# A GRU scan on one core: the candidate's second products with both state halves at once, the low half of r times h ahead of the update gate's additions, and the conditions' products one pair later

## What is computed

```python
xz, xr, xh = x @ W_z, x @ W_r, x @ W            # for all steps
vz, vr, vh = cond @ C_z + b_z, cond @ C_r + b_r, cond @ C + b   # once
def step(h, xs):
    z = sigmoid(xz_t + h @ U_z + vz)
    r = sigmoid(xr_t + h @ U_r + vr)
    hh = tanh(xh_t + (r * h) @ U + vh)
    return (1 - z) * h + z * hh
```

## Time and profile before

| | before |
|---|---|
| median of 3 runs | 1507.63 us |
| the profiled execution | 1507.41 us, span 1505.6 us |
| PE busy | 1499.5 us, 22917 matmuls |
| PEld busy | 1173.5 us, 98 ns for one fp16 load |
| DVE busy | 1259.6 us |
| ACT busy | 1173.0 us |
| POOL busy | 315.4 us |
| granted TensorE clock | full speed (2.4 GHz) in every slice |

### The profile page before, as it was taken

The page is one execution under the profiler, slowest core; times in us unless marked ns, Lnnn a source line. Parts: engine busy times, 40 slices in busy tenths (PEclk is TensorE's granted clock), DMA queues, the critical chain, the costliest instruction groups (busy, mean ns, idle before and its releaser), DMA issues.

```text
span 1505.6 us, 54107 instructions
## 1 busy us (share of the span) xinstructions
PE 1499.5 (100%) x22917; PEld 1173.5 (78%) x22917; DVE 1259.6 (84%) x2548; ACT 1173.0 (78%) x2726; POOL 315.4 (21%) x332
## 2 busy tenths in 40 slices
PE   9999999999999999999999999999999999999998
PEld 7874444444444467779999999999999999999998
DVE  7999999999999887777877787778887887776677
ACT  7989999999999835767777777777777777867444
POOL 1100112111110014322222222222222222222222
PEclk9999999999999999999999999999999999999999
DMA  5156465565638979533333333333333333320000
GB/s 199 40 157 194 90 192 140 133 160 142 182 87 133 143 113 102 72 53 23 49 20 48 48 21 48 42 27 47 21 47 48 20 49 20 49 41 3 32 32 31
DMA packets 545106, 116.61 MB, mean 77 GB/s; under 512 B 520160, under 2 KB 527200, under 8 KB 536160
## 3 DMA queue, kind: packets, MB, share of 16 engines
q1 hardware_dynamic: 537424, 82.14, 31.4%
q0 software_dynamic: 7008, 30.41, 11.0%
q10 hardware_dynamic: 432, 0.59, 0.1%
HBM read 66.47 MB, written 33.55 MB: 66 GB/s over the span
## 4 chain that ended last, share of the span: by engine, by line
PE 99%; DVE 0%; issue 0%; ACT 0%; DVEq 0%
PE ps L1553 33%; PE ps L1618 22%; PE ps L1655 20%; PE ps L1667 15%; PE ps L1639 6%; PE ps L1571 2%; PE ps L1510 0%; PE ps L1520 0%; PE ps L1584 0%; DVE ST L1382 0%; DVE AR L1349 0%; ACT ST L943 0%; DVE RL L1439 0%; DVE HL L981 0%; DVE HL L1486 0%
## 5 line engine op out<-in xcount | busy, mean ns | idle before, releaser
L1553 PE MATMUL ps<-XH,WH 128*128 128x512 f16 x1872 | 404.7, 379 | 0.0
L1553 PEld LDWEIGHTS ps<-XH,WH 128*128 128x128 f16 x1872 | 182.9, 98 | 220.2 <-issue 0.3
L1655 PE MATMUL ps<-HL,U 128*128 128x64 f16 x6112 | 219.8, 193 | 0.6 <-ACT ps L775 0.6
L1779 POOL TENSOR_TENSOR ST<-ST 128x256 f32<-128x256 f32 x126 | 114.5, 908 | 491.1 <-ACT ST L935 491.1
L1667 PE MATMUL ps<-HL,U 128*128 128x64 f16 x4064 | 213.9, 206 | 0.0
L1655 PEld LDWEIGHTS ps<-HL,U 128*128 128x128 f16 x6112 | 203.6, 98 | 7.1 <-ACT ps L775 0.7
L1667 PEld LDWEIGHTS ps<-HL,U 128*128 128x128 f16 x4064 | 183.1, 98 | 0.1
L1655 PEld LDWEIGHTS ps<-RL,U 128*128 128x128 f16 x4064 | 135.1, 98 | 6.1 <-issue 0.8
L1655 PE MATMUL ps<-RL,U 128*128 128x64 f16 x4064 | 139.2, 193 | 0.0
L903 ACT ACTIVATE ST<-ps,dn 128x128 f32<-128x128 f32 x252 | 78.1, 360 | 70.4 <-PE ps L1667 70.4
L950 ACT ACTIVATE HL<-ST 128x128 f16<-128x128 f32 x208 | 53.3, 302 | 80.4 <-DVE ST L1478 80.4
(11 more groups left out here) (215 smaller groups left out, 3116.4 us busy)
## 6 DMA issues: line engine op xcount, KB each, us to landing
x_scratch<-AR SPq DMA_DIRECT2D x16, 1024.0 KB, 5.3
AR<-in_x POOLq DMA_DIRECT2D x15, 1024.0 KB, 8.1
AR<-HB POOLq DMA_DIRECT2D x11, 1024.0 KB, 7.0
raw<-x_scratch SPq DMA_DIRECT2D x88, 128.0 KB, 4.4
out_y<-raw SPq DMA_DIRECT2D x11, 1024.0 KB, 4.1
raw<-in_x SPq DMA_DIRECT2D x10, 1024.0 KB, 7.4
ST<-in_x SPq DMA_DIRECT2D x5, 1024.0 KB, 7.2
out_y<-AR SPq DMA_DIRECT2D x4, 1024.0 KB, 4.2
```

The costliest lines, as they stand in the source:

```text
L1553: op = pe.matmul(ps[b][:, :], v[:, g, wp, k, e * P:(e + 1) * P], y[:, xp, k, :], start=n == 0, stop=n == 11)
L1655: pe.matmul(ps[b][:, col:col + B], U[:, g, half, k, e * P:(e + 1) * P], S[:, k, 0], start=opens, stop=False, skip_group_check=True)
L1779: pool.tensor_tensor(zc, zc, Hst[(t + 1) % 2], ALU.mult).then_inc(s_zch, 1)
```

## The change

Three edits.

1. In steps 16 to 119 C takes the joint form too (`summed_pair`): 16 matmuls of 64 columns with the low weights, then 16 of 128 columns with the high weights and both halves of `RL`. The two parts of a sum lie side by side in PSUM. `put_x` writes half the projection into both parts (512 elements of a partition, not 256). DVE adds the parts (`add_pair`, a `tensor_reduce` with two elements in each sum, one for each bank) into SBUF, and ACT takes tanh from there with the same scale. `add_pair` stands in DVE's list behind the side work of the middle of the step.
2. In steps 8 to 111 DVE makes the low half of r*h ahead of the two additions of Z.
3. `C_PAIR` is {14, 18, 22}: the conditions' products stand one pair later.

```diff
-        C_PAIR = {13: 1, 17: 2, 21: 0}
+        C_PAIR = {14: 1, 18: 2, 22: 0}
...
-            return g == 0 and not held(t, g)
+            return g == 0 and not held(t, g) or summed_pair(t, g)
...
+        def summed_pair(t, g):
+
+            return g in SUMMED and SUMMED_FROM <= t < HELD_TO
...
+                if summed_pair(t, g):
+                    both = PS[:, first * 512:(first + 2) * 512].rearrange("p (e s b) -> p e s b", e=KT, b=B)[:, :, 0:2]
+                    x = XP[j % 2][:, g, :, tt * B:(tt + 1) * B].unsqueeze(2).to_broadcast([P, KT, 2, B])
+                    act.activation(both, x, ACT.Copy, scale=uh[:, 3 + g:4 + g]).then_inc(s_put[g], 1)
+                    return
...
+                        if summed_pair(t, 2):
+                            act.wait_ge(s_pc, 2 * sums_by_dve(t, 2) - 1 + h)
+                            act.activation(two(hg, h), two(hg, h), ACT.Tanh, scale=dn[:, scale(5)]).then_inc(s_hh, 1)
...
+            def add_pair(dst, banks, done, sums):
+
+                for h in range(2):
+                    dve.wait_ge(*sums[h])
+                    dve.tensor_reduce(two(dst, h), pairs(banks[h]), AX.X, ALU.add).then_inc(done, 1)
...
-                if halved_by_act(t):
-                    dve.wait_ge(s_Z, u + 1)
-                    add_x(t, zg, Z, 0, (0, 1, 2, 3), s_zh, s_pz, u + 1)
-                else:
+                if not halved_by_act(t):
                     dve.tensor_tensor(rf, rg, Hp, ALU.mult).then_inc(s_rf, 1)
                 dve.wait_ge(s_rhi, 2 * u + 2)
                 dve.wait_ge(s_rf, made(t))
                 dve.tensor_tensor(rlo, rf, rhi, ALU.subtract).then_inc(s_rlo, 1)
-                if not halved_by_act(t) and not held(t, 0):
+                if not held(t, 0):
                     dve.wait_ge(s_Z, u + 1)
                     add_x(t, zg, Z, 0, (0, 1, 2, 3), s_zh, s_pz, u + 1)
...
+                if summed_pair(t, 2):
+                    add_pair(hg, C, s_pc, [(s_C, 2 * u + 1), (s_C, 2 * u + 2)])
...
-                per = 2 * B if joint else B
+                per = 4 * B if summed_pair(t, g) else 2 * B if joint else B
+                n = 2 * B if joint else B
```

More of the change, by code:

```diff
@@ L35 @@
 HELD_FROM, HELD_TO = 2, 15 * 8
+SUMMED_FROM, SUMMED = 2 * 8, (2,)
 QUICK = 3
@@ L111, in build @@
         mx, ag, ee, er, up, dn = (sb(n, 15 + NCH) for n in ("mx", "ag", "ee", "er", "up", "dn"))
-        dx1, ux1, bound, dc, uh = sb("dx1", 3), sb("ux1", 3), sb("bound", 4), sb("dc", 3), sb("uh", 4)
+        dx1, ux1, bound, dc, uh = sb("dx1", 3), sb("ux1", 3), sb("bound", 4), sb("dc", 3), sb("uh", 6)
         dx = sb("dx", 3 * NCH)[:, :].rearrange("p (c g) -> p c g", g=3)
@@ L390, in is_joint, with by_dve @@
         def is_joint(t, g):
-            return g == 0 and not held(t, g)
+            return g == 0 and not held(t, g) or summed_pair(t, g)
         def held(t, g):
             return t == T - 1 or g == 1 and t >= HELD_FROM or g == 2 and HELD_FROM <= t < HELD_TO
+        def summed_pair(t, g):
+            return g in SUMMED and SUMMED_FROM <= t < HELD_TO
+        def by_dve(t, g):
+            return not held(t, g) or summed_pair(t, g)
         def puts(t, g):
@@ L402, in sums_by_dve @@
         def sums_by_dve(t, g):
-            return sum(not held(n, g) for n in range(1, t + 1))
+            return sum(by_dve(n, g) for n in range(1, t + 1))
         def halved_by_act(t):
@@ L415, in held_sums, with pairs @@
             return ps[b][:, 0:2 * B].rearrange("p (e b) -> p e b", e=2)
+        def pairs(b):
+            return ps[b].rearrange("p (e s b) -> p e b s", e=2, b=B)[:, :, :, 0:2]
         def z_sums():
@@ L764, in put_x @@
                 if puts(t, g) == 1:
-                    act.wait_ge(s_ux1, 5)
+                    act.wait_ge(s_ux1, 7)
                 if j == 0:
@@ L776, in put_x @@
                     return
[L777 to L780, removed]
+                if by_dve(t - 1, g):
+                    act.wait_ge(s_pr if g == 1 else s_pc, 2 * sums_by_dve(t - 1, g))
                 else:
@@ L900, in _ @@
                     for h in range(2):
-                        if held(t, 1):
+                        if summed_pair(t, 1):
+                            act.wait_ge(s_pr, 2 * sums_by_dve(t, 1) - 1 + h)
+                            act.activation(two(rg, h), two(rg, h), ACT.Sigmoid, scale=dn[:, scale(4)]).then_inc(s_r, 1)
+                        elif held(t, 1):
                             act.wait_ge(s_R, 2 * u + h + 1)
@@ L940, in _ @@
                     for h in range(2):
-                        if held(t, 2):
+                        if summed_pair(t, 2):
+                            act.wait_ge(s_pc, 2 * sums_by_dve(t, 2) - 1 + h)
+                            act.activation(two(hg, h), two(hg, h), ACT.Tanh, scale=dn[:, scale(5)]).then_inc(s_hh, 1)
+                        elif held(t, 2):
                             act.wait_ge(s_C, 2 * u + h + 1)
@@ L1427, in _ @@
                     dve.tensor_scalar(uh[:, 3:4], dn[:, scale(3)], -1.0, None, ALU.mult).then_inc(s_ux1, 1)
+                    for g in (1, 2):
+                        dve.tensor_scalar(uh[:, 3 + g:4 + g], up[:, scale(3 + g)], 0.5 * HS, None, ALU.mult).then_inc(s_ux1, 1)
                     evacuate_first(t)
@@ L1430, in _ @@
                     continue
+                if summed_pair(t, 1):
+                    add_pair(rg, R, s_pr, [(s_R, 2 * u + 1), (s_R, 2 * u + 2)])
                 for h in range(0 if held(t, 1) else 2):
@@ L1666, in recurrent_second @@
                         closes = k == KT - 1 and (e % 2 == 1 if split else e == KT - 1)
-                        op = pe.matmul(ps[b][:, col:col + per], U[:, g, 0, k, e * P:(e + 1) * P],
+                        op = pe.matmul(ps[b][:, col:col + n], U[:, g, 0, k, e * P:(e + 1) * P],
                                        S[:, k] if joint else S[:, k, 1], start=False, stop=closes, skip_group_check=True)
```

## The result

| | before | after |
|---|---|---|
| median of 10 runs | 1507.74 us (1507.57 to 1508.08) | 1511.22 us (1510.92 to 1511.66) |
| ratio | 1 | 1.0023, 95% interval 1.0015 to 1.0032 |
| span of the profiled execution | 1505.6 us | 1509.4 us |
| PE busy | 1499.5 us, 22917 matmuls | 1499.4 us, 21253 matmuls |
| DVE busy | 1259.6 us | 1318.3 us |

The kernel is slower, as forecast, but by 3.5 us where 9.8 were forecast (1517.4). The range held it.

A forecast was written before the change was run, and what follows sets the result against it. PE was taken to bound the whole scan. From 1507.41 us, savings of 5.2, carried waits of 13.2 and step 16's 1.8 gave 1517.2, and 0.2 for the median made 1517.4 us; range 1502 to 1522.5.

The forecast's parts named there:

- C's fixed cost: C on PE: the fixed cost of 16 matmuls saved, 0.04 us a step, -4.2 us over 104 steps.
- order, steps 8 and 9: C on PE in steps 8 and 9: 0.15 us less waiting each for the low half of r*h, -0.3 us.
- place 1, 11 steps: Second step of each chunk: r begins about 0.8 us later, so PE waits 0.17 us for the high half.
- place 2, 11 steps: Place 2 of each chunk: lateness carried from place 1 makes PE's wait grow from 0.3 to 0.7 to 0.85 us.
- place 3, 11 steps: Place 3 of each chunk: starts without slack, side work late; PE waits 0.37 us or less, 0.3 in the chunk's sum.
- step 16: Step 16: no slack, r late by ACT's longer write, Z's sums wait for the low half; about +1.8 us.
- steps 112 to 127: End of the scan: steps 112 to 119 lose about 0.24 us of a slack of about 0.4, costing nothing.
- The wait of place 2 on its own, 0.3 us: Place 2, nothing carried in: 0.9 us added to the chain against 0.58 us of slack, PE waits 0.3 us.
- waits only where the slack is short by itself: Rival: place 2 waits 0.3 us in 11 steps, step 16 1.8 us, nothing carried; 1507.5 us, chance 0.18.
- The additions are not hidden: Denies a rival: DVE's reductions of C are hidden, only the savings are left; 1502.4 us, chance 0.20.
- DVE is not the bound: Denies a rival: with 0.6 us reductions every place but 4 and 6 waits; 1524 us, chance 0.07.
- The wide matmuls are not spaced by their loads: Denies a rival: C's 128-column matmuls each wait for their own 98 ns weight load; +70 us, chance 0.01.

The follow-up runs named there:

- e7: The kernel after, with C in its old form in place 1 of each chunk: 1508.05 us, ratio 1.0001.
- e3: The kernel after, with the joint form of C only in places 2 and 3 of each chunk and in steps 112 to 119: 1508.36 us, ratio 1.0006.
- e1, experiment 1: The kernel after without the joint form of C; the new DVE order and the conditions one pair later stay: 1507.43 us, ratio 0.9998.
- e2: The kernel after, with Z's sums again ahead of the low half of r*h: 1532.47 us, ratio 1.0164.
- e8: The kernel after, with one extra r times h of 0.33 us on DVE ahead of the two L1199, place 2 of 11 chunks: 1517.99 us, 1.0068 of before.
- e9: The kernel after, with one extra reduction of 0.33 us on DVE behind the two L1199, place 2 of 11 chunks: 1514.12 us, 1.0042 of before.
- e4, experiment 5: The kernel after, with one L1199 instead of two ahead of the reductions in places 2 and 3, others at step ends: 1505.78 us, ratio 0.9987.

## Why the prediction was right or wrong

| step of the sum | forecast us | measured us |
|---|---|---|
| C's fixed cost | -4.2 | -4.2 |
| the conditions | -0.7 | -0.9 |
| first 7 us of the span | 0 | +0.3 |
| order, steps 8 and 9 | -0.3 | +0.3 |
| place 1, 11 steps | +1.9 | 0.0 |
| place 2, 11 steps | +8.2 | +2.5 |
| place 3, 11 steps | +3.3 | +2.6 |
| step 16 | +1.8 | +1.6 |
| step 110 | 0 | +0.2 |
| steps 112 to 127 | 0 | +1.2 |
| sum | +9.8 | +3.8 |

The measured rows are made with the -0.04 of every step taken out; 3.8 is the difference of the spans, and the rounded rows come within 0.2 of it. The forecast rows add up to 10.0: the prediction rounded a chunk's 1.22 us to 1.2. It also wrote 1.8 for step 16, whose terms are 1.1 + 0.6.

**What bounds the kernel, and by which mechanism it slows: right.** PE saved what was counted in C, 0.04 us a step, and the waits of places 2 and 3 against it stand in no list of waits. The added serial part is where it was put, behind the side work, and the wait of place 2 is carried there from place 1 (e7, e3). r*h in place 2 began 2.21 to 2.31 us into the step (forecast 2.3), the side work 4.32 to 4.42 (4.47).

**The term that failed: place 2, 0.75 us a step where 0.23 was measured.** The forecast's chain gave 4.47 + 1.59 + 2.13 + 0.15 = 8.34 us against a step of 7.50, 0.84 us, and 0.75 was taken. Step 42 has 4.35 + 1.17 + 2.06 + 0.14 = 7.72: 0.22 us. First, I kept the two L1178 at the 1.59 us of the earlier trace rows; they take 1.17. The row's own mean of the two hides that one took 0.68 and the other 1.07, so I didn't ask why, and the reason, GpSimd's start, is moved by the very edit that was costed (e1, e2, e8, e9). That is 0.42 us, the larger part. Second, the side work began 0.12 us earlier than forecast. Third, the reductions: 0.47 us and 0.39 to the next by the nearest row, 0.42 and 0.33 measured, 0.11 us together, of which the instructions behind them give back 0.04. With GpSimd's start where it had been, the change would have cost 0.36 x 11 = 4.0 us more, about 1515: an estimate from e8 and e9.

**The wait of place 2 on its own, 0.3 us: wrong**; it has none (e3, e7). With the two L1199 at their old length it would have one: e2's step is 7.99 us long for its high half, where 7.50 needs none, and the new order brings the side work 0.27 us forward (4.22 to 3.95), which leaves 0.22. So the rival "waits only where the slack is short by itself" (1507.5) was nearer in time than the forecast, but its mechanism is the one that fell.

**The reduction.** A row that I had passed by would have given it: a reduction of 256 elements from SBUF in the kernel before (busy us, mean ns | idle before):
```profile
L1009 DVE TENSOR_REDUCE bound<-CT 128x1 f32<-128x256 f32 x1 | 0.4, 410 | 0.0
```
It is 410 ns, as the 2048-element rows gave by proportion. I added for PSUM, and PSUM costs next to nothing here (418). The bound of 0.6 us "if short inner loops cost extra" came from no row, and no run shows it. The Trainium skill's figure ("VectorE: DVE Perf Modes", errata), 0.39 us by an estimate from its 120 cycles, was nearer than my row of 483 ns; the rule itself lies under both measured rows that read PSUM (418 and 483 ns).

**Place 1: 0.17 us forecast, 0.02 at most measured.** Its high half is ready just in time: 7.47 us into step 25 by the trace, where I had 7.63, 0.14 us ahead of R. In the other chunks it is 0.14 to 0.25 us ahead, and places 2 and 3, which wait, have 0.14. Since a place that is just in time carries nearly as much as one that waits, the chain into place 2 held all the same.

**Steps 8 and 9, and 110 to 119: sign and zero wrong.** In steps 8 and 9 I costed the instruction that moved and not the queue that it was moved past. The low half takes with it a wait for ACT's high half, and all behind it, Z's sums first, comes 0.79 us later (experiment 1). In steps 112 to 119 the second products of R wait 0.08 to 0.14 us each for the low half of h; e1, without the joint form, has 0.04 us in one step. I had called 0.24 us of 0.4 us of slack harmless. Step 110 waits 0.22 us for its high half: r's sigmoids begin 2.31 us into it, 1.56 before, behind side work of 1.22 us on ACT and the longer write. That the miss was not larger is luck: these steps and 126 cost 2.0 us more than the forecast had for them, against 8.3 us less in places 1 to 3.

**The other rivals.** The additions are not hidden: places 0, 1 and 4 to 7 hide them, 2 and 3 don't. DVE is not the bound: it is busy for 87% of the span, and six of eight places don't wait. The wide matmuls are not spaced by their loads: 56 ns each in C as in Z.

**What stays open.** Step 126, one of the last, is 0.35 us longer in after, and in e2 and e4, though none of the edits touches it (the 0.23 us of e8 are another wait, for the low half of h). In these three DVE's first addition of C begins 4.94 to 4.95 us into the step; in the kernels without the extra time it begins at 4.59 to 4.60, 0.03 us ahead of a GpSimd product; that product begins at 4.62 to 4.63 in both groups. Whether the two are connected no run tests. Nor do I know why the first 7 us of the span vary by 0.4 us.

## What to carry to other kernels

Before a duration is carried over from a trace, look at each instruction behind the mean: where two of a kind differ, something beside them sets the time, and the edit may move that too. Work added behind an engine's side work costs nothing up to the slack and nearly one for one from there, and a place that ends with none hands its lateness to the next. Here it was enough to leave one piece of side work ahead of the additions in places 2 and 3 and to move the others to the ends of steps (experiment 5, 5.4 us); a shorter addition was not tried. When an instruction is moved ahead of another on the same engine, its own wait moves as well, and everything behind it pays for that.

## What the runs showed of the hardware

- DVE and GpSimd at one time, both with two operands in SBUF: the one that begins first runs at its own speed and the other is held up. DVE 0.67 us and GpSimd 0.99 where DVE began first; DVE 1.01 to 1.07 and GpSimd 0.73 where GpSimd did, 0.05 to 0.12 us ahead. Moving a start by 0.33 us was worth 0.35 us (e8 against after). The reduction from PSUM (0.33 us to the next, 754.38 to 754.72) was not held up by an L1810 that ran beside it.
- A reduction of 256 elements takes 418 ns from PSUM and 410 ns from SBUF; the one from PSUM lets the next start after 0.33 us.
- Joint products of 128 columns take 56 ns each in C as in Z, in a stream where each has a weight load of 98 ns of its own, against 29 ns for 64 columns.
